# Decoder layer, attention stage: the sums over values of two heads in one stream, masked probabilities in two buffers, three output banks

## The reference

```python
# L0_attn: x (2, 512, 1024), 32 query heads, 8 key/value heads, depth 128, window 128
q = (x @ wq.T); k = (x @ wk.T); v = (x @ wv.T)       # split into heads
s = einsum('bhgnd,bhmd->bhgnm', qg, k) / sqrt(128)
mask = (j <= i) & (i - j < 128)
p = softmax(where(mask, s, -inf))
o = einsum('bhgnm,bhmd->bhgnd', p, v)
x = layernorm(x + o @ wo.T)
# L0_xattn: both operands quantised to 0..255 (x and the 1024 context rows of a batch), one matrix product
x = layernorm(x + fake_quant(x) @ fake_quant(ctx))
# L0_ffn: gate and up product, silu, truncation to whole numbers, down product
x = layernorm(x + ffn(x))
```

## Time and profile before

| | us |
|---|---|
| median of three runs | 1490.64 (1489.87 to 1491.8) |
| profiled execution | 1492.75, of this span 1491.0 |
| PE busy in the span | 1443.0 (97%) |
| DVE, ACT, POOL busy | 989.6, 786.5, 740.1 |
| attention slots of PE | 437.5 to 1018 |
| mean granted TensorE clock | 0.992 of 2.4 GHz |

### The profile page before, as it was taken

How to read it: one execution, slowest core, us unless ns; L and a number is a source line. 1 busy time by engine, 2 the same in 40 slices (tenths; PEclk the granted TensorE clock), 3 DMA queues, 4 the chain that set the end, 5 groups by cost and what they waited for, 6 DMA issues and landing times.

```text
span 1491.0 us, 23433 instructions
## 1 busy us (share of the span) xinstructions
PE 1443.0 (97%) x7332; PEld 1176.6 (79%) x7349; DVE 989.6 (66%) x1768; ACT 786.5 (53%) x1561; POOL 740.1 (50%) x651
## 2 busy tenths in 40 slices
PE   8899999999999999999999999999889999999996
PEld 6688888888878888888888888887557887877642
DVE  7644444445566577778777777886777565656598
ACT  5433333333445375656565666663566555555574
POOL 0477777776566444555455554553575333344000
PEclk9999999999999999999999999999989999999998
DMA  6477777777652857575766666670131222222611
GB/s 226 159 276 273 273 273 278 281 282 271 222 198 78 309 174 269 193 274 188 258 224 245 225 211 233 240 272 32 43 127 71 92 98 91 86 71 83 226 43 72
DMA packets 105883, 281.12 MB, mean 189 GB/s; under 512 B 12768, under 2 KB 13152, under 8 KB 105824
## 3 DMA queue, kind: packets, MB, share of 16 engines
q1 hardware_dynamic: 105824, 280.41, 53.6%
HBM read 184.94 MB, written 95.42 MB: 188 GB/s over the span
## 4 chain that ended last, share of the span: by engine, by line
PE 43%; DVE 12%; ACT 5%; issue 4%; DMA 4%; POOL 1%; SPq 0%; DVEq 0%; ACTq 0%; POOLq 0%
PE ps L1082 6%; PE ps L1083 6%; PE ps L1084 6%; PE ps L1244 5%; PE ps L1245 5%; PE ps L1033 2%; PE ps L1034 2%; PE ps L1035 2%; DMA f_raw<-w_down 2%; PE ps L1167 2%; PE ps L1064 1%; PE ps L1065 1%; DVE u_val L2751 1%; PE ps L1046 1%; PE ps L1063 1%
## 5 line engine op out<-in xcount | busy, mean ns | idle before, releaser
L1014 PE MATMUL ps<-xo_h,wb_h 128*128 128x512 f32 x644 | 251.4, 390 | 5.9 <-ACT c L1462 2.5
L1015 PE MATMUL ps<-xo_l,wb_h 128*128 128x512 f32 x644 | 250.7, 389 | 0.0
L1016 PE MATMUL ps<-xo_h,wb_l 128*128 128x512 f32 x644 | 250.6, 389 | 0.0
L2089 POOL TENSOR_TENSOR pm_l<-pt_l,upto 128x512 fp32r<-128x512 f32 x64 | 82.4, 1287 | 251.5 <-DVE pt_l L2413 251.5
L1082 PE MATMUL ps<-wo_h,o_h 128*128 128x512 f32 x512 | 206.3, 403 | 0.0
L1083 PE MATMUL ps<-wo_l,o_h 128*128 128x512 f32 x512 | 199.8, 390 | 0.0
L1084 PE MATMUL ps<-wo_h,o_l 128*128 128x512 f32 x512 | 199.6, 390 | 0.0
L1457 ACT ACTIVATE wb_h<-wf_l 128x512 fp32r<-128x512 f32 x69 | 43.6, 632 | 197.0 <-DVE wf_l L2342 81.7
L1014 PEld LDWEIGHTS ps<-xo_h,wb_h 128*128 128x128 f32 x644 | 120.9, 188 | 33.7 <-issue 5.9
L2062 POOL TENSOR_TENSOR wb_l<-wf_l,wb_h 128x512 fp32r<-128x512 f32 x66 | 87.8, 1330 | 112.0 <-DVE s_sum L2337 56.6
L1506 ACT ACTIVATE prob<-prob,exp_bias 128x128 f32<-128x128 f32 x256 | 99.8, 391 | 78.4 <-DVE exp_bias L2400 78.4
(11 more groups left out here) (252 smaller groups left out, 3656.9 us busy)
## 6 DMA issues: line engine op xcount, KB each, us to landing
raw<-w_att SPq DMA_DIRECT2D x47, 512.0 KB, 5.4
f_raw<-w_gu SPq DMA_DIRECT2D x44, 512.0 KB, 5.1
u_gu<-f_unit SPq DMA_DIRECT2D x42, 512.0 KB, 4.5
gq<-u_gu SPq DMA_DIRECT2D x42, 512.0 KB, 3.9
wp_raw<-w_att SPq DMA_DIRECT2D x32, 512.0 KB, 5.8
wo_high<-wp_h SPq DMA_DIRECT2D x32, 512.0 KB, 2.8
wo_low<-wp_l SPq DMA_DIRECT2D x32, 512.0 KB, 4.1
q_rows<-c SPq DMA_DIRECT2D x64, 256.0 KB, 2.8
```

The costliest lines, as they stand in the source:

```text
L1014: pe.matmul(prod_ps[i], wh, chunk(xo_h[i], c), start=(i in OPENS and c == 0), stop=False, skip_group_check=True)
L1015: pe.matmul(prod_ps[i], wh, chunk(xo_l[i], c), start=False, stop=False, skip_group_check=True)
L1016: last = pe.matmul(prod_ps[i], wl, chunk(xo_h[i], c), start=False, stop=(c == KH - 1), skip_group_check=True)
```

## The change

1. `values_pair(g, j)` takes the place of `values` from unit 6 of group 0 on. It runs in odd slots only, for units j-3 and j-2, which share their values: one weight load serves both heads' probabilities. Key blocks 0 and 1 of the first two query blocks go to one bank (5), the rest to another (1). The moving operands are 512 columns or two pieces of 128 columns.
2. `sums_high_pair`, `sums_low_pair` on ACT and DVE: two instructions of 2 x 256 columns each in odd slots, none in even slots.
3. `pm_h` and `pm_l` get a second buffer for the odd units. Room for it comes from the context's second raw buffer: `ctx_raw` has one buffer, so each context load waits until the tile before is quantised. In the last group the loads stand in slots 0, 2, 3, 4 (before: two in slot 0, two in slot 2).
4. The output product rotates over three banks (0, 6, 7) in the place of four (0, 1, 6, 7).
5. Behind the last group `values(6)` goes, and `values(7)` becomes `values_pair(6)`.

```diff
-        pm_h = place("pm_h", [P, TPB, 2, P], F32R)
-        pm_l = place("pm_l", [P, TPB, 2, P], F32R)
+        pm_h = place("pm_h", [P, 2, TPB, 2, P], F32R)
...
-        ctx_raw = place("ctx_raw", [P, 2, KCTX], F32, at_r4 + 32768)
+        ctx_raw = place("ctx_raw", [P, KCTX], F32, at_r4 + 32768)
+        pm_e = place("pm_e", [P, TPB, 2, P], F32R, at_pm + 4096)
+        pm_l = place("pm_l", [P, 2, TPB, 2, P], F32R, at_r4 + 36864)
...
-        y_ps = [bank(0), bank(1), bank(6), bank(7)]
+        oq_ps = [bank(i).rearrange("p (h k) -> p h k", h=2) for i in (5, 1)]
+        y_ps = [bank(0), bank(6), bank(7)]
+        Y_BANK = (0, 1, 2, 0, 1, 2, 0, 1, 2, 0, 1, 2, 0, 1, 2, 1)
...
             def load_context(k, odd):
-                if isinstance(k, int):
-                    wait(sp, ctx_quant, k - 1)
-                sp.dma_start(ctx_raw[:, odd, :], ctx_rows[k]).then_inc(ctx_loaded[odd], 16)
+                wait(sp, ctx_quant, k)
+                sp.dma_start(ctx_raw[:, :], ctx_rows[k]).then_inc(ctx_loaded[odd], 16)
...
-                if not first and j in (0, 2):
-                    if last:
-                        for odd in range(2):
-                            load_context(2 * (HKV - 2) + j + odd, odd)
-                    else:
-                        load_context(g * 2 + (j // 2 - 2), j // 2)
+                if last and j in (0, 2, 3, 4):
+                    k = 2 * (HKV - 2) + max(j - 1, 0)
+                    load_context(k, k % 2)
+                if not first and not last and j in (0, 2):
+                    load_context(g * 2 + (j // 2 - 2), j // 2)
...
+            def values_pair(g, j):
+
+                n = g * UNITS + j
+                par, b, h = unit(j)
+                pe.wait_ge(p_masked, n + 2)
+                wait(pe, o_low, n)
+
+                def into(dst, a, first, wide, start, stop):
+                    vh = v_h[b][:, a, :]
+                    vl = v_l[b][:, a, :]
+                    ph = pm_h[:, :, a, first:first + wide, :]
+                    pl = pm_l[:, :, a, first:first + wide, :]
+                    pe.matmul(dst, vh, ph, start=start, stop=False, skip_group_check=True)
+                    pe.matmul(dst, vh, pl, start=False, stop=False, skip_group_check=True)
+                    return pe.matmul(dst, vl, ph, start=False, stop=stop, skip_group_check=True)
+
+                low, high = oq_ps
+                into(low[:, :, 0:2 * P], 0, 0, 2, True, False)
+                into(low[:, :, P:2 * P], 1, 0, 1, False, True).then_inc(pv_done, 1)
+                into(high[:, :, 0:P], 1, 1, 1, True, False)
+                into(high[:, :, 0:2 * P], 2, 0, 2, False, False)
+                into(high[:, :, P:2 * P], 3, 0, 1, False, True).then_inc(pv_done, 1)
...
             # slot_of on PE; ACT and DVE have the same form with sums_high_pair and sums_low_pair
-                if not first or j >= 2:
+                if first and j >= 2:
                     values(g, j - 2)
+                if not first and j % 2 == 1:
+                    values_pair(g, j - 3)
...
             # mask_probs on POOL
-                wait(pool, pv_done, n)
+                if isinstance(g, int) and g == 0 and j < SINGLES:
+                    high, low = pm_h[:, 0], pm_e
+                    wait(pool, pv_done, n)
+                else:
+                    high, low = pm_h[:, j % 2], pm_l[:, j % 2]
+                    wait(pool, pv_done, g * UNITS + j // 2 * 2)
...
+            def sums_low_pair(g, j):
+                n = g * UNITS + j
+                par, b, h = unit(j)
+                for i in range(2):
+                    rows = slice(i * 2 * P, (i + 1) * 2 * P)
+                    dve.wait_ge(o_high, n + (i + 1))
+                    dve.tensor_tensor(o_l[b][:, h:h + 2, rows], oq_ps[i], plain(o_h[b][:, h:h + 2, rows]),
+                                      ALU.subtract).then_inc(o_low, 1)
```

More of the change, by code:

```diff
@@ L529, in out_block, with y_turn, y_since @@
             return 0, 0, 2 * (j - 6) + k, 0
+        SINGLES = 6
+        def y_turn(j, k):
+            return (2 * j + k + 4) % 16
+        def y_since(j, k):
+            turn = y_turn(j, k)
+            return next(d for d in range(1, 16) if Y_BANK[(turn - d) % 16] == Y_BANK[turn])
         def late_product(event):
@@ L1099, in out_slot @@
                     pe.wait_ge(wo_loaded[1], g * 32 + 32)
-                out_product(g * 16 + (2 * j + k - 12), y_ps[(2 * j + k) % 4], t, half)
+                m = g * 16 + (2 * j + k - 12)
+                wait(pe, y_added, g * 16 + (2 * j + k - 11 - y_since(j, k)))
+                out_product(m, y_ps[Y_BANK[y_turn(j, k)]], t, half)
             def out_tile(t):
@@ L1108, in out_tile @@
                     pe.wait_ge(y_added, m - 1)
[L1109 removed]
+                    out_product(m, y_ps[1 + half], t, half)
             def slot_of(g, j, first, last):
@@ L1229, in _ @@
             out_tile(3)
-            values(g, 7)
+            values_pair(g, 6)
             sum_context(1, 0)
@@ L1553, in scale_context @@
                 act.wait_ge(ctx_loaded[odd], loads * 16)
-                act.activation(ctx_raw[:, odd, :], ctx_raw[:, odd, :], ACT.Relu,
+                act.activation(ctx_raw[:, :], ctx_raw[:, :], ACT.Relu,
                                bias=param(Z2), scale=param(R2)).then_inc(ctx_scaled, 1)
@@ L1559, in quantise_context @@
                 act.wait_ge(ctx_rounded, k + 1)
-                act.activation(ctx_q[:, k if isinstance(k, int) else bass.ds(k, 1), :], ctx_raw[:, odd, :], ACT.Identity,
+                act.activation(ctx_q[:, k if isinstance(k, int) else bass.ds(k, 1), :], ctx_raw[:, :], ACT.Identity,
                                bias=param(UNROUND)).then_inc(ctx_quant, 1)
@@ L1579, in slot_of @@
                     late(event)
-                if not first or j >= 2:
+                if first and j >= 2:
                     sums_high(g, j - 2)
+                if not first and j % 2 == 1:
+                    sums_high_pair(g, j - 3)
                 if first and j == 1:
@@ L2487, in slot_of @@
                     late(event)
-                if not first or j >= 2:
+                if first and j >= 2:
                     sums_low(g, j - 2)
+                if not first and j % 2 == 1:
+                    sums_low_pair(g, j - 3)
                 if not first or j >= 1:
```

33 lines of the change are left out of this document (19 added, 14 removed).

## The result

The changed kernel takes 1499.52 us (median of five runs, 1496.44 to 1502.01), the kernel before on the same chip 1489.87 (five runs). The ratio is 1.0062, with a 95% interval of 1.0051 to 1.0073: 9.65 us slower. The forecast was 1496.7, slower by 6.1. The profiled execution of the changed kernel took 1502.01 us, with a span of 1500.3; it is the slowest of its five, and some 1.2 us of its distance to the profile before lie ahead of attention, where nothing was changed.

The account below looks back on a forecast made before the run. The attention loop looked bound by PE, but pairs (-7.8) and transposes' waits (+3.1, +5.3) gave +0.6; the last group added +0.3 and +5.2: +6.1 us on 1490.64, so 1496.7 us, with an 8-in-10 range of 1489.5 to 1502.

Parts of the forecast that it names:

- Pairs, -7.8 us: PE's values blocks: a pair takes 2.43 us instead of 2.70, saving 0.27 on each of 29 pairs, 7.8 us less.
- Rival 3: A moving operand in two pieces costs as two matmuls: 17.7 us on top, 1514.4 us; chance 4%.
- Rival 4: Cost per matmul is small, so merging saves nothing on PE: 7.2 of 7.8 us fail to come, 1503.9 us; 5%.
- Slot 4, +3.1: Slot 4 of groups 1 to 6: value transposes newly wait 0.51 us for DVE's `pt_l`, +3.1 us.
- Slot 0, +5.3: Slot 0 of seven groups: value transposes wait for `pt_l`, each group paying 0.75 us, +5.3 us.
- Slot 4 of the last group, +0.3: Late context tiles delay ACT's score copy; transposes wait 1.1 to 2.8 us, against 1.6 before: +0.3 us.
- Slot 6, +5.2: Last group: context tile 15 lands late behind `wo`, so PE waits around slot 6's start for `q_low` and `o_l`: +5.2 us.
- Rival 2: The context tile behind `wo` is hidden: only +0.9 us, 1491.5 us, within 0.2%; chance 17%.
- The clock: If slot 6's wait of 5 us let PE's clock fall, that would come on top; no size in the sum.

Follow-up runs that it names:

- filler: Changed kernel with two more 512-column matmuls, result overwritten, in the second output product of slots 0 and 4 of groups 1 to 7: 1498.66 us.
- early: Changed kernel with the copy of transposed probabilities (`pt_l`) put first on ACT and DVE in slots 0 and 4 of groups 1 to 7: 1486.95 us.
- before_early: Kernel before the change, with the transposed probabilities (`pt_l`) made early in slots 0 and 4: 1485.79 us.
- ctx_ahead: Changed kernel with the load of context tile 15 in slot 4 of the last group issued ahead of the 1 MB `wo` loads: 1493.50 us.
- ctx_alone: Kernel before the change, with only the context edit: one raw buffer and the new places of the loads, no pairs: 1497.71 us.
- both: Changed kernel with the early `pt_l` in slots 0 and 4 and context tile 15 loaded ahead of `wo`: 1483.02 us.
- prm: Changed kernel with four small parameter loads issued in slot 2 of group 0 instead of slot 7: 1495.75 us.
- all3: Changed kernel with early `pt_l` in slots 0 and 4, context tile 15 ahead of `wo`, parameters loaded in slot 2 of group 0: 1481.86 us.

## Why the prediction was right, and where it was off

- **Direction and mechanism: right.** The loop looks bound by PE and is not: saving 0.27 us on each pair only moved PE onto the next chain. *filler* shows that it waits there, *early* that this chain is what costs, *before_early* that without it the 0.27 come in.
- **Pairs, -7.8 us: right.** 2.44 us a pair (2.43), two-piece matmuls 0.118 apart (0.119). Rival 3 is out. Rival 4 is out too: *before_early* against *early* gives 0.27 us a pair. By the gaps of the Trainium skill ("TensorE: Matmul & The Clock Gate", section "Back-to-back issue gap"), an estimate, a pair would be 2.28 us, which the measured 2.44 does not bear out.
- **Slot 4, +3.1: right** (+3.2). Slot 4's wait is 0.54 us for 0.51.
- **Slot 0, +5.3: mis-sized, +6.4.** I moved DVE's row as a block, anchored to PE. Its check is anchored to POOL's product too, and that moved by 0.22 us relative to the slot. Two steps failed: "so it gains only the `o_l` that goes" looked at DVE alone, and "Odd slots grow by 1.08 us on PE and by 0.60 on DVE", costed at nothing, was 1.30 on DVE in slot 7, 0.70 of it beside POOL.
- **Slot 4 of the last group, +0.3: right** within its bounds (copy at 2.77 us, forecast 2.7 to 4.4; wait 1.7 for 1.1 to 2.8). The old wait was taken as 1.6 from the list's idle time; by starts, as the new one was counted, it is 1.7, so the term should have read +0.2, and it measured 0.0.
- **Slot 6, +5.2: right in its chain, mis-sized, +3.5.** The tile was there 9.8 us behind `wo`'s issue, not 11.3. I took the time of `u_gu`, which stood at the same place, right behind the 2 MB, but carries data out to HBM: 10.2 us from issue to landing, and the tile 8.6. Why it took longer stays open. *ctx_ahead* takes all of it away, and *ctx_alone* shows that this part costs some 6 us even without pairs. Rival 2 (hidden) is out.
- **The clock: +3.1 that were not in the sum.** The last sentence of the prediction named the case of slot 6. It came there, 1.7 us, and in group 1 besides, 1.4. To leave it out of the sum was the largest error: in *ctx_alone* it is about half of the loss. A wait of over 2 us on PE should have carried a price of its own.
- **The rest.** The terms as measured, without the clock, give -7.8 + 3.2 + 6.4 + 3.5 = +5.3; with it +8.4. The medians differ by 9.65. The missing 1.2 us are of the size of the runs' spread (5.6 us) and I don't assign them.

What stays open is the stage behind attention. It was not edited, and from slot 7 of the last group to the end it took 480.2 (before_early) to 488.8 us (both) in the profiles, 484.9 in the kernel before and 486.1 in the changed one. With single profiles I can't say how much of it follows from what attention leaves behind. The clock goes with it: from 1060 to 1130 us the mean granted clock was 0.98 in *early*, *before_early* and *prm*, whose stage took 480.2 to 481.7 us, and 0.90 to 0.95 in the other eight, with 483.3 to 488.8; 0.08 of 70 us is 5.6 us of work at the full rate. This limits every comparison of two spans; the medians are what counts.

## What to carry to other kernels

Before saving work on an engine that is busy for 97%, find in each kind of slot the next chain that ends there and its distance to the engine; here it was 0.24 us, and an edit of 1.35 us per slot ran into it. Then move that chain first: the places of two instructions were worth 12.6 us, where the work saved was 7.8. And when a buffer is given away, look at what stands ahead of its loads in the DMA queue at the one place where they come in a row.

## What the runs showed of the hardware

**The clock does not follow the length of a wait alone.** It fell to 1.2 GHz behind PE waits of 2.31 us (changed kernel), 2.77 (around its end, *both*), 2.31 (*ctx_alone*), and did not behind one of 2.28 in the same slot 0 of group 1 of *ctx_ahead*:

```profile
526.00:528.00 2.00, 1.10 (x10) 1.13 (x11) 1.35 (x3) 0.36 (x1) 1.09 (x1) 1.00 0.70 270
```

Nor did it behind the wait of 1.9 us for `wo_l` in *all3*. In *early* it fell behind 2.30 and 2.23 us with a block of scores between them. The plainest case is slot 4 of group 0, where every kernel here waits for the value transposes, by 1.65 to 1.68 us. In ten of the eleven profiles the clock stayed up behind that wait; in *early* it fell, to 0.50 in the stretch 490 to 492 us:

```profile
488.99 0.63 PE L1108 MATMUL ps<-ident,v_raw 128*128 128x128 f32 x4 [1.65 <-DVE pt_l L2471]
```

So the same wait can cost a spell in one execution and none in the next.

**A matmul's start-to-start time at the lower level.** Timeline of the changed kernel in its second spell:

```profile
1008.42 0.63 PE L1118 MATMUL ps<-wo_l,o_h 128*128 128x512 f32 x1
...
1010.12 0.63 PE L1119 MATMUL ps<-wo_h,o_l 128*128 128x512 f32 x1
```

(1010.12 - 1008.42) / 4 = 0.425 us for 512 columns, against 0.227 at the upper level: a factor of 1.87 and not 2. Half of 0.425 is 0.213, so a matmul takes 0.014 us more at the upper level than halving gives. The Trainium skill, "TensorE: Matmul & The Clock Gate", section "Wait — 56ns, not 53.3ns?", gives 426.7 ns at 1.2 GHz and 215.7 at 2.4 for this size; the rows agree with the first and not with the second.

**POOL and DVE hold each other up in both directions.** In *early*, DVE's normalisation took 1.56 us (alone 0.69) behind a product of POOL that itself took 2.32 (alone 1.28) beside DVE's check:

```profile
767.22 2.32 POOL L2147 TENSOR_TENSOR pm_l<-pt_l,upto 128x512 fp32r<-128x512 f32 x1 [1.76 <-DVE pt_l L2471]
```

Each ends about its own time behind the end of the other: 768.41 + 1.28 = 769.69, shown 769.54; 769.54 + 0.69 = 770.23, shown 770.10. An instruction moved on one of them moves the other.
